# A state-space block on one core: the third tile of the first half takes its carried part on VectorE, and four orders change

## The reference

```
u   = layernorm(groupnorm(x))                 # fx: per group of 3 channels, then over the 96 channels
Bu  = B_bar u ;  xs[t] = lam_bar * xs[t-1] + Bu[t]      # 48 complex states = 96 real rows
y   = 2 Re(C xs) + D * u
y   = gelu(y) + u
fy  = layernorm(y)
z1, z2 = W_enc fy ;  z = z1 * gelu(z2)
out = x + W_dec z + fy
```

## Time and profile before

| | |
|---|---|
| median of 3 runs | 97.53 us (97.2 to 97.99) |
| the profiled execution, its own time | 97.87 us |
| its span in the profile | 96.0 us |
| PE busy | 88.8 us (93%) |
| DVE busy | 69.1 us (72%) |
| ACT, POOL busy | 46.2 us, 34.8 us |

### The profile page before, as it was taken

How to read it: one execution, slowest core, us unless ns; L and a number is a source line. 1 busy time by engine, 2 the same in 40 slices (tenths; PEclk the granted TensorE clock), 3 DMA queues, 4 the chain that set the end, 5 groups by cost and what they waited for, 6 DMA issues and landing times.

```text
span 96.0 us, 1476 instructions
## 1 busy us (share of the span) xinstructions
PE 88.8 (93%) x484; PEld 52.7 (55%) x484; DVE 69.1 (72%) x223; ACT 46.2 (48%) x98; POOL 34.8 (36%) x56
## 2 busy tenths in 40 slices
PE   5999989999999989998999999989999999999930
PEld 3667857776775647765667446653425425333310
DVE  1477898899878997575994338899504999975570
ACT  3450019998695491170486396730894220232200
POOL 7902068890059800500055000059950000990000
PEclk9999999999999999999999999999999999999999
DMA  1999300000000000000000000000000003530244
GB/s 41 221 280 257 86 3 0 0 7 0 0 0 0 3 0 7 0 0 0 0 0 3 0 0 7 0 0 0 0 0 0 0 0 84 163 87 0 82 118 128
DMA packets 3783, 3.79 MB, mean 39 GB/s; under 512 B 512, under 2 KB 3680, under 8 KB 3776
## 3 DMA queue, kind: packets, MB, share of 16 engines
q1 hardware_dynamic: 3520, 3.68, 14.5%
q10 hardware_dynamic: 256, 0.02, 0.2%
HBM read 2.12 MB, written 1.57 MB: 38 GB/s over the span
## 4 chain that ended last, share of the span: by engine, by line
PE 73%; DVE 12%; ACT 8%; issue 2%; DVEq 1%; ACTq 0%
PE ps L531 73%; ACT sq L446 3%; ACT xc L448 2%; DVE rs L802 2%; ACT xc L428 2%; DVE fy L802 1%; ACT ps L459 1%; DVE sq L802 1%; DVE y L1074 1%; DVE rs L832 1%; DVE fx L802 1%; ACT y L481 1%; DVE rs L807 1%; DVEq L91 1%; DVE upper L806 0%
## 5 line engine op out<-in xcount | busy, mean ns | idle before, releaser
L531 PE MATMUL ps<-wm 96*96 96x256 f32 x50 | 15.3, 463 | 1.2 <-DVE wm L1044 1.2
L531 PE MATMUL ps<-fy,mt 96*96 96x512 f32 x32 | 14.9, 600 | 0.7 <-DVE fy L802 0.7
L378 POOL TENSOR_TENSOR res<-fy,xs 96x512 f32<-96x512 f32 x8 | 10.0, 1277 | 10.7 <-DVE fy L802 10.6
L481 ACT ACTIVATE y<-ps,vecs 96x512 f32<-96x512 f32 x8 | 5.5, 685 | 15.6 <-PE ps L531 15.6
L370 POOL TENSOR_TENSOR y<-gl,fx 96x512 f32<-96x512 f32 x4 | 5.1, 1286 | 21.1 <-DVE parts L802 11.7
L531 PEld LDWEIGHTS ps<-wm 96*96 96x96 f32 x50 | 9.5, 201 | 4.6 <-DVE wm L1044 1.2
L802 DVE SCALAR_TENSOR_TENSOR w<-ps,vecs,y 96x512 f32<-96x512 f32 x8 | 5.9, 744 | 7.4 <-ACT y L481 7.4
L531 PEld LDWEIGHTS ps<-fy,mt 96*96 96x96 f32 x32 | 5.0, 163 | 8.1 <-issue 6.3
L531 PE MATMUL ps<-fx,um 97*96 97x256 f32 x32 | 8.4, 390 | 0.2 <-DVE fx L802 0.2
L531 PE MATMUL ps<-xs,pm 96*96 96x256 f32 x32 | 8.0, 387 | 0.4 <-DVE pm L890 0.4
L531 PE MATMUL ps<-w,yl 96*96 96x256 f32 x32 | 8.0, 381 | 0.2 <-ACT ps L459 0.2
(11 more groups left out here) (123 smaller groups left out, 158.8 us busy)
## 6 DMA issues: line engine op xcount, KB each, us to landing
out_dram<-sq SPq DMA_DIRECT2D x7, 192.0 KB, 2.2
xs<-x_dram SPq DMA_DIRECT2D x3, 384.0 KB, 6.7
xs<-x_dram SPq DMA_DIRECT2D x2, 192.0 KB, 3.1
mt<-mats_dram SPq DMA_DIRECT2D x1, 338.6 KB, 7.3
out_dram<-sq SPq DMA_DIRECT2D x2, 96.0 KB, 2.1
mt<-mats_dram SPq DMA_DIRECT2D x1, 180.0 KB, 5.5
sm<-small_dram ACTq DMA_DIRECT2D x1, 9.8 KB, 2.8
cmask<-mask_dram ACTq DMA_DIRECT2D x1, 9.0 KB, 3.4
```

The source lines that it names most:

```text
L378: nc.gpsimd.tensor_tensor(cols(res, H, i), cols(fy, H, i), xs[:, HB * H + 2 * i:HB * H + 2 * i + 2, :].rearrange("c n l -> c (n l)"), ALU. ...
L481: nc.scalar.activation(cols(gz, H, i), bank(*Z2[H, i])[0:96, :], ACT.Gelu, bias=vecs[:, 1:2]).then_inc(gz_ready, 1)
L531: return nc.tensor.matmul(o, lhsT, rhs, start=start, stop=stop)
```

## The change

Seven edits, of four kinds.

1. The carried part of tile 2 of half 0 moves from PE to DVE. PE loses two matmuls (`carried_outputs(0, 2)`), and `local_outputs(0, 2)`, two matmuls, moves from before seed_sum(0) to after the carried parts of tiles 0 and 1. DVE gets `complete(0, 4)` and `complete(0, 5)`: four completes now stand between the scans 2 to 6 of half 1 where two stood. The counts of w_full rise by 2.
2. Statistics: `statistics(1, 0)` moves from before group_norm(0) to after its deviations, one more stays behind it (six instead of five), and PE's group_mean(1) moves behind one more centering matmul.
3. PE's inputs(0, 0) moves ahead of eight of the matmuls of variances(0, 1, .).
4. ACT's direct_term(0, 1) moves ahead of two of its four evacuations.

```
--- before.py
+++ after.py
@@ -507,8 +507,9 @@
             first_state(0)
             centered_values(1, 2, 4)
             direct_term(0, 0)
-            centered_values(1, 4, HB)
+            centered_values(1, 4, 6)
             direct_term(0, 1)
+            centered_values(1, 6, HB)
             direct_term(0, 2)
             seed(0)
             first_state(1)
@@ -689,7 +690,7 @@
             center_batch(0, 1)
             group_bias(0)
             for n in range(2, HB):
-                if n == 5:
+                if n == 6:
                     group_mean(1)
                 center_batch(0, n)
             group_variance(1)
@@ -719,18 +720,18 @@
             pe.wait_ge(bcm_ready, 1)
             broadcast(0, 0)
             variances(0, 1, 0)
-            variances(0, 1, 1)
             pe.wait_ge(ones_ready, 1)
             for i in range(NT):
-                if i < 2:
-                    variances(0, 1, i + 2)
+                if i == 1:
+                    for j in range(1, NT):
+                        variances(0, 1, j)
                 if i == NT - 1:
                     open_bank(0, 0)
                 inputs(0, i)
             open_bank(0, 1)
             pe.wait_ge(dm_ready, 1)
             pe.wait_ge(yl_ready, 1)
-            for i in range(NT - 1):
+            for i in range(NT - 2):
                 pe.wait_ge(direct_ready, i + 1)
                 local_outputs(0, i)
                 if i == 0:
@@ -742,10 +743,14 @@
                 doubling(0, i)
             direct(0, NT - 1)
             pe.wait_ge(yl_ready, 2)
-            for i in range(NT - 1):
+            for i in range(NT - 2):
                 open_bank(1, i)
                 carried_outputs(0, i)
+            pe.wait_ge(direct_ready, NT - 1)
             pe.wait_ge(w_full, RT)
+            local_outputs(0, 2, True)
+            open_bank(1, 2)
+            pe.wait_ge(w_full, 2 * RT)
             local_outputs(0, NT - 1, True)
             for i in range(2):
                 pe.wait_ge(direct_ready, NT + i)
@@ -763,10 +768,10 @@
             for i in range(2):
                 carried_outputs(1, i)
             pe.wait_ge(direct_ready, 2 * NT - 2)
-            pe.wait_ge(w_full, 2 * RT)
+            pe.wait_ge(w_full, 3 * RT)
             local_outputs(1, 2, True)
             direct(1, NT - 1)
-            pe.wait_ge(w_full, 3 * RT)
+            pe.wait_ge(w_full, 4 * RT)
             local_outputs(1, NT - 1, True)
             broadcast(1, 0)
             encode(0, 0)
@@ -1048,11 +1053,10 @@
                 statistics(0, q)
                 step_chain_on(1)
             dve.wait_ge(in_early, 16)
-            statistics(1, 0)
-            group_norm(0, lambda j: step_chain_on(1), lambda: (statistics(1, 1), statistics(1, 2)))
+            group_norm(0, lambda j: step_chain_on(1), lambda: (statistics(1, 0), statistics(1, 1)))
             for n in range(FIRST_PM):
                 scale_centering(0, n)
-            for q in range(3, HB):
+            for q in range(2, HB):
                 statistics(1, q)
                 step_chain_on(1)
             group_norm(1, lambda j: step_chain_on(1), lambda: step_chain_on(5))
@@ -1086,8 +1090,8 @@
                 doubled(0, i)
             for b in range(1, T):
                 scan(1, b)
-                if b in (2, 3):
-                    complete(0, T - 4 + b)
+                if b in (2, 3, 4, 5):
+                    complete(0, T - 2 * RT + b - 2)
             second_input(0, 1)
             second_input(0, 3)
             for k in range(NDBL):
```

## The result

The changed kernel takes 98.05 us (median of 22 executions, 97.41 to 98.68); the kernel before, run beside it as often, 97.68 (97.03 to 98.59). The ratio is 1.0048, with a 95% interval of 1.0027 to 1.0068: slower by about half a percent, clear of no change though under the 1% bound. The forecast was +0.55 us on 97.53, 98.1. The profiled execution took 98.35 us, with a span of 96.5 (96.0 before). Medians in this document are over all executions of a kernel; the ratios leave out those more than 1.5% above the fastest of the same kernel.

A forecast was written before the change was run, and what follows sets the result against it. PE, busy 93% of the span, seemed the bound, but DVE's `parts` held the broadcast of half 1. Broadcast +0.08 and held complete +0.47 gave +0.55 us on the median 97.53, 98.1 us; 8-in-10 range 96.9 to 98.6.

The forecast's parts named there:

- The removed pair: Before half 1's broadcast: 0.87 us less PE work buys at most 0.16 us, since the broadcast waits for DVE's `parts`.
- The rival that counted PE's work in full: Utmost of the faster case: PE's work alone counts and both waits go, 96.5 us; faster case's chance 0.14.
- The statistics: DVE's chain to `parts` of half 0 gets 0.24 us later, bounds 0 and 0.45, passed on to half 1's broadcast.
- The prediction put this at nothing: Inputs ahead of variances and the earlier direct term: both hidden, 0; PE's work up to the variance unchanged.
- Taking them away brings nothing there: Moving statistics from before group_norm(0) gains 0.05 us at most, since DVE waits there for PE's mean until 9.92.
- a gain in executions with a later load: Part of the faster rival: executions with a later load gain 0.2 to 0.4 us from the statistics; chance 0.14.
- Together: At half 1's broadcast: removed pair and statistics sum to +0.08 us, 38.43 instead of 38.35, bounds -0.16 and +0.29.
- The held complete: Fourth complete of half 0, blocked by POOL's addition, ends at 49.88; PE's last local pair +0.47 us, bounds 0 and +0.61.
- What follows: Behind the last local pair of half 0: scans 6 and 7 and second_input(0, 3) arrive in time, nothing else added.
- the signs to look for: Profile marks: seed sum near 36.5, PE idle 0.8 to 1.0 us, broadcast 38.4, fourth complete 1.3 to 1.5 us.
- The granted clock: Rival: PE's idle before the broadcast drops its clock to 1.2 GHz, adding 1.5 to 4 us; slower case's chance 0.08.

The follow-up runs named there:

- early completes: Changed kernel with half 0's four completes one scan earlier, behind scans 1 to 4 of half 1: 97.38 us, ratio 0.9975 to the kernel before.
- old statistics: Changed kernel with completes one scan earlier and statistics(1, 0) back ahead of the group norm: 97.67 us, ratio 1.0003 to the kernel before.
- the three orders: Orders of statistics, inputs and direct term; run alone, as the changed kernel with tile 2's carried part back on PE: 97.52 us, ratio 1.0003.
- the kernel before with the split: Kernel before with POOL forming yl blocks 0 to 5 and two rotX matrices early, the rest behind `parts`: 97.43 us, ratio 0.9984.
- the repeated split kernel: Second run of the changed kernel with completes one scan earlier and part of POOL's yl and rotX work behind `parts`: 96.53 us, ratio 0.9854.
- the gap-filled one: Changed kernel with two unused 96x256 matmuls between seed sum and broadcast of half 1: 98.45 us (four executions), ratio 1.0112 to the kernel before.
- the split kernel: Changed kernel, completes one scan earlier, POOL forming yl blocks 0 to 3 and two rotX matrices early, the rest behind `parts`: 96.28 us, ratio 0.9864.
- POOL waits: Changed kernel with POOL's first addition of half 0 waiting for the last complete: 97.41 us, ratio 0.9982 to the kernel before.
- the four with the split: Runs with POOL's yl and rotX work split: changed kernel with completes earlier (0.9864, again 0.9854), kernel before (0.9984), orders alone (0.9902).

## Why the prediction was right

Each term can be read off the table, and the sum holds: in the profiles 0.09+0.44 = 0.53 us against the forecast 0.55. The two medians differ by 0.37 only, the ratio stands for 0.47 (0.26 to 0.66). That the absolute forecast, 98.1, was met so closely has luck in it: the kernel before was 0.15 slower over 22 executions than over the three at hand, which made up for most of the difference.

- *The removed pair* was to buy 0.16 us at the broadcast, for DVE ends `parts` then. Alone it bought 0.14 (24.49 to 24.35), and with the early completes, the old statistics and the two other orders 0.16 (24.33). Filling the gap with 0.86 us of other work moved nothing. The rival that counted PE's work in full is out.
- *The statistics* were to delay DVE's chain by 0.24. From pm of half 0 to the start of `parts` of half 1 it takes 37.93-13.76 = 24.17 instead of 37.78-13.86 = 23.92, 0.25. The size is right, but one link of the account is wrong. The row in which DVE reads the variance of half 1 comes only 0.06 later behind pm (17.04 against 16.98), because the orders of inputs and direct term bring it 0.19 sooner: with them and the old statistics it comes at 16.79. The prediction put this at nothing, for PE's work up to the variance was unchanged. What hides it is POOL, which starts yl when `parts` of half 0 is there, 0.26 later behind pm, and so holds DVE's int32 instruction until 0.25 later. The changed kernel, DVE then POOL:

```profile
30.80 0.29 DVE L812 TENSOR_SCALAR rs<-ps 128x128 f32<-128x128 f32 x1 [0.16 <-PE ps L532]
31.53 0.90 DVE L812 TENSOR_SCALAR rs<-rs 128x128 int32<-128x128 int32 x1
30.53 1.81 POOL L361 TENSOR_TENSOR yl<-yl 96x768 f32<-96x768 f32 x1
```

  The runs bear this out: with the earlier reading at 16.79 `parts` starts at the same 23.92 behind pm, and with POOL out of the way the three orders together delay it by 0.06 to 0.07 only (23.04 and 23.05 against 22.98 in the kernel before with the split).

  "Taking them away brings nothing there" held only for an execution like the profiled one, whose warm-up ended at 9.65. In a short one it brings about 0.3 us. The forecast had that as a gain in executions with a later load; there the load did come later (9.69 against 9.45), and the mean was there 0.65 earlier (9.27 against 9.92), which uncovers the wait. Over all executions the orders come out at nothing: ratio 1.0003.
- *Together* +0.08 at the broadcast was forecast, +0.09 measured (24.58 against 24.49).
- *The held complete* was to end at 49.88 (49.96 with the +0.08) and cost PE 0.47. It ended at 49.86 in an execution 0.1 us ahead, and cost 11.57-11.13 = 0.44. Two edits that keep it out of POOL's way, one on DVE's side and one on POOL's, give 0.46 and 0.47 back.
- *What follows* was to pass the sum on unchanged: from the last local pair to the end of the span it is 96.0-49.48 = 46.5 before and 96.5-49.91 = 46.6 after.
- *Of the signs to look for*, the seed sum near 36.5 (36.44), the idle time of 0.8 to 1.0 (0.84) with DVE as releaser, the broadcast at 38.4 (38.34), the complete of 1.3 to 1.5 (1.40), a PE wait of about 0.5 behind it (0.47 by the step) and the seed sum of half 1 at 51.7 (51.71) are all there. The granted clock did go below 1.00, but only in the last half microsecond.

The Trainium skill's rule (SBUF — State Buffer, Who interferes with whom) that a DVE instruction with two SBUF inputs and a GpSimd instruction that reads SBUF exclude one another, the first to start going through, agrees with all runs here, in both directions. The held int32 `rs` has one input in SBUF only, so in this kernel two such inputs are not the whole condition. The figure that the same page gives for a descriptor write held by VectorE, the other's end plus 0.115 us (section A bandwidth-pool intuition that's wrong (but worth ruling out)), would, applied here, have put the complete's end at 49.58+0.115+0.47 = 50.17. It ended at 49.86, as if its 0.47 us had begun 0.19 before POOL's recorded end.

## What to carry to other kernels

Before moving work off the busiest engine, look at what that engine waits for next: if it is another engine's result, the saved time turns into idle time there, and the place to work on is the other engine's chain. Before adding an instruction to VectorE, list where its inputs lie and what GpSimd runs at the moment of its issue: here the same instruction cost nothing at 47.6 and 0.93 us at 48.5. A chain that another engine holds takes its time from that engine: here DVE read the variance 0.19 us sooner and got nothing for it, for POOL still held the next instruction. And a saved piece that is worth little can become worth more later, once the wait behind which it was hidden is shortened.

## What was not expected of the hardware

PE's 12 warm-up matmuls at the start, released at 1.19 us in every profile, took between 7.27 and 8.62 us from execution to execution. The rows of the shortest and of the longest, from the repeated split kernel and from the gap-filled one:

```profile
1.19 7.27 PE L539 MATMUL ps<-wm 96*96 96x256 f32 x24 [1.19 <-DVE wm L1057]
```

```profile
1.19 8.62 PE L532 MATMUL ps<-wm 96*96 96x256 f32 x24 [1.19 <-DVE wm L1051]
```

The single records of these rows in the traces show how this comes about. In every profile they first follow each other at 0.43 us, and from one moment on at 0.22: a matmul, two records, costs 0.85 us and then 0.43, as at 1.2 and at 2.4 GHz. The moment is 4.98 us in the first of the two and 7.69 in the second (7.70 in the kernel before), after PE had worked without a break from 1.19. Half of the 2.71 between them is the difference of the two rows. The trace's own record of the granted clock, 1.00, begins at that same moment; ahead of it there is none, and the views show 1.00 there too. So the first nines of the page, in the earlier trace rows as well, do not show a full clock, and PE's steps show half of it. What sets the moment the runs do not show.

It moves all that follows. In the two profiles of the split kernel the warm-up took 7.90 and 7.27, pm came at 13.14 and 12.58, and the spans are 93.9 and 93.3. A second, smaller scatter lies at the end: behind the issue of the last stores the span goes on for 3.0 us in five profiles (POOL waits and the four with the split) and for 3.3 in the other eight; the cause is not shown, and a part of what the medians of those kernels show may come from it. Together this sets a limit: a term of 0.1 us is seen in a profile from a common event, not in 22 executions of each kernel.
